# A graph network on one core: the lookup of 40 of 125 edge columns by TensorE taken out of the graph convolutions

## What is computed

```python
def gcn_conv(x, edge_index, W, b, num_nodes):
    ...
    norm = dinv[src_f] * dinv[dst_f]
    h = x @ W
    msg = h[src_f] * norm[:, None]
    out = jax.ops.segment_sum(msg, dst_f, num_segments=num_nodes)
    return out + b
```

## Time and profile before

| | |
|---|---|
| median of 3 runs | 33,800.93 us |
| range of the runs | 33,789.78 to 33,812.31 us |
| span of the profiled execution | 36,520.8 us |
| busy, share of the span: TensorE (PE) | 39% |
| VectorE (DVE) | 44% |
| ScalarE (ACT) | 7% |
| GpSimd (POOL) | 66% |
| mean granted TensorE clock | 0.635 |

### The profile page before, as it was taken

The page is one execution under the profiler, slowest core; times in us unless marked ns, Lnnn a source line. Parts: engine busy times, 40 slices in busy tenths (PEclk is TensorE's granted clock), DMA queues, the critical chain, the costliest instruction groups (busy, mean ns, idle before and its releaser), DMA issues. The chain is left out here.

```text
span 36520.8 us, 282841 instructions
## 1 busy us (share of the span) xinstructions
PE 14234.9 (39%) x71326; PEld 10717.5 (29%) x71326; DVE 16109.6 (44%) x34560; ACT 2593.5 (7%) x3901; POOL 24245.9 (66%) x29018
## 2 busy tenths in 40 slices
PE   1111100211110166664666524444444344266664
PEld 1111100111110155553555413222223222144443
DVE  3333337233333576663666513333334343344443
ACT  0000000000000000000000001001001000133230
POOL 6888841677774366664666566777687866477773
PEclk5555555555555577776778756666666666677775
DMA  2111112111112211110111110000000000100001
GB/s 49 15 15 15 15 37 106 19 23 21 23 23 52 89 29 29 28 29 14 29 29 30 24 11 10 13 10 10 12 11 13 11 12 8 60 14 15 14 14 51
DMA packets 1089471, 937.07 MB, mean 26 GB/s; under 512 B 580669, under 2 KB 1031893, under 8 KB 1063893
## 3 DMA queue, kind: packets, MB, share of 16 engines
q1 hardware_dynamic: 440100, 695.25, 6.4%
q0 software_dynamic: 646368, 201.76, 5.8%
q10 hardware_dynamic: 1872, 28.29, 0.2%
HBM read 497.08 MB, written 426.83 MB: 25 GB/s over the span
## 5 line engine op out<-in xcount | busy, mean ns | idle before, releaser
L1177 POOL DMA_INDIRECT messages<-se_M,se_rstage x2625 | 3029.5, 1154 | 1757.1 <-DVE se_M L1547 956.0
L1177 POOL DMA_INDIRECT messages<-pe_M,pe_rstage x2625 | 3132.7, 1193 | 1072.2 <-issue 791.8
L527 POOL DMA_INDIRECT se_G<-tab,se_stage x3125 | 3225.9, 1032 | 785.6 <-issue 783.3
L527 POOL DMA_INDIRECT g2g_G<-tab,g2g_stage x3125 | 3006.8, 962 | 1060.9 <-issue 779.0
L527 POOL DMA_INDIRECT g1g_G<-tab,g1g_stage x3125 | 3252.2, 1041 | 596.2 <-issue 582.3
L495 POOL DMA_INDIRECT c1c_G<-tab,c1c_stage x2125 | 2520.5, 1186 | 659.0 <-issue 640.0
L495 POOL DMA_INDIRECT c2c_G<-tab16b,c2c_stage x2125 | 2486.1, 1170 | 659.0 <-issue 640.8
L1076 DVE SCALAR_TENSOR_TENSOR g2gh_junk<-g2gh_pB,g2gh_src_f,earlier 128x128 f32<-128x128 f32 (+4 forms) x2625 | 1455.9, 614 | 2586.3 <-remote 1502.7
L1492 DVE TENSOR_TENSOR se_V<-se_pTV,s_b 128x160 f32 (+1 forms) x625 | 202.6, 324 | 4875.4 <-remote 3064.0
L767 PE MATMUL g1gh_acc<-g1gh_oh_hi,g1gh_oh_lo 128*128 128x100 bf16 x6250 | 546.5, 282 | 4133.4 <-DVE g1gh_oh_hi L747 3965.8
L1581 PE MATMUL se_pTV<-ident,se_pair 128*32 128x128 f32 x3125 | 598.3, 338 | 3904.0 <-DVE se_pair L1488 2600.5
(11 more groups left out here) (617 smaller groups left out, 36219.7 us busy)
## 6 DMA issues: line engine op xcount, KB each, us to landing
scans<-g1w_W SPq DMA_DIRECT2D x25, 3187.5 KB, 9.9
c1cm_row<-match SPq DMA_DIRECT2D x500, 128.0 KB
c2cm_row<-match SPq DMA_DIRECT2D x500, 128.0 KB
edges<-g2g_G SPq DMA_DIRECT2D x25, 2062.5 KB
g2w_G<-edges SPq DMA_DIRECT2D x25, 2062.5 KB, 11.6
scans<-g2w_W SPq DMA_DIRECT2D x25, 2062.5 KB, 7.3
g1g_G<-tab,g1g_stage POOLq DMA_INDIRECT x3125
g2g_G<-tab,g2g_stage POOLq DMA_INDIRECT x3125
```

Source lines behind the costliest of these rows:

```text
L527: g.indirect_dma_start(out=G[b][:, t, :], out_offset=None, in_=table, in_offset=bass.IndirectOffsetOnAxis(ap=stage[b][:, t:t + 1], axis=0) ...
L1177: g.indirect_dma_start(out=view, in_=M[b][:, DC + t, :], in_offset=None, out_offset=bass.IndirectOffsetOnAxis(ap=stage[b][:, t:t + 1], axis=0)
```

## The change

`gcn_gather` no longer makes a `Match`. All 125 columns are gathered by GpSimd through `stage_first` and `gather_and_stage`, as in `gat_gather`. VectorE and TensorE keep the side work alone, SP keeps the stores. Class `Match`, `match_rows`, the DRAM tensors `match` and the constants go.

```diff
-def gcn_gather(k, name, table, values, left, scans, carry, side):
+def gcn_gather(k, name, table, scans, carry, side):
...
-        stage = [c.sb(f"{name}_stage{b}", [P, PCH], I32) for b in range(2)]
+        stage = [c.sb(f"{name}_stage{b}", [P, CH], I32) for b in range(2)]
...
-        match = Match(k, c, name + "m", left)
         with k.nc.Block() as block:
             @block.gpsimd
             def _(g):
-                over_chunks(g, lambda i, b, j: gather_column_loop(
-                    g, k, i, j, b, table, G, stage, staged, stored, 16, got, k.src_i, PCH))
+                def chunk(i, b, j, first=False, last=False):
+                    gather_and_stage(g, i, j, b, table, G, stage, staged, stored, 16, got, k.src_i,
+                                     first=first, last=last)
+                stage_first(g, stage, staged, k.src_i)
+                chunk(0, 0, 0, first=True)
+                with g.Fori(0, PAIRS - 1) as j:
+                    chunk(2 * j + 1, 1, j)
+                    chunk(2 * j + 2, 0, j + 1)
+                chunk(NCH - 2, 1, PAIRS - 1)
+                chunk(NCH - 1, 0, PAIRS, last=True)
...
                 def chunk(i, b, j):
-                    match.heat(v, i, 0)
-                    v.wait_ge(stored[b], (j + 1) * 16)
-                    for m in range(max(NB + 1, side.groups)):
-                        if 1 <= m <= NB:
-                            match.mask(v, i, m - 1)
-                        if m + 1 < NB:
-                            match.heat(v, i, m + 1)
-                        if m < side.groups:
-                            side.vector(v, ch, i, side.ranges[0][0] + m)
-                        if 1 <= m <= NB:
-                            match.empty(v, G[b], i, m - 1)
-                    v.wait_ge(match.emptied, (i + 1) * NB + 2)
-                    v.wait_ge(got[b], (j + 1) * (16 * PCH))
+                    for m in range(side.groups):
+                        side.vector(v, ch, i, side.ranges[0][0] + m)
+                    v.wait_ge(got[b], (j + 1) * (16 * CH))
...
-            match_rows(k, "mr")
...
-            gcn_gather(k, name + "c", table, xs[:, :, :], agg, scan16, carry, side)
+            gcn_gather(k, name + "c", table, scan16, carry, side)
```

More of the change, by code:

```diff
@@ L45 @@
 D = 16
[L46 to L52, removed]
 H1, C1 = 3, 32
@@ L1012, in _ @@
             def _(pe):
-                match.tensor_first(pe)
                 side.tensor_first(pe)
                 def chunk(i, b, j):
[L1017 to L1025, removed]
+                    for m in range(side.groups):
+                        side.tensor_rows(pe, i, side.ranges[0][0] + m)
+                        side.tensor(pe, i, side.ranges[0][0] + m, False)
                 over_chunks(pe, chunk)
@@ L1035, in _, with chunk @@
                     s.sem_inc(stored[b], 16)
[L1037 to L1040, removed]
+                def chunk(i, b, j):
                     s.wait_ge(scanned, i + 1)
                     s.dma_start(rows(scans)[:, cols(i), :], G[b][:, :, :]).then_inc(stored[b], 16)
[L1043 to L1048, removed]
+                over_chunks(s, chunk)
                 s.wait_ge(stored[0], 16 * (PAIRS + 2))
@@ L1179, in scatter_column_loop @@
                              ).then_inc(sent[b], 16)
[L1182 to L1192, removed]
-            @block.tensor
-            def _(pe):
-                pe.wait_ge(staged, 1)
-                for i in range(NCH):
-                    mm = pe.transpose(turned[:, i * P:(i + 1) * P], src_f[:, i, :], k.ident[:, :])
-                mm.then_inc(transposed, 1)
-            @block.vector
-            def _(v):
-                ch = Chain(v, step)
-                v.tensor_copy(src_f[:, :, :], k.src_i[:, :].rearrange("p (i c) -> p i c", c=CH)[:, :, PCH:CH]
-                              ).then_inc(staged, 1)
-                v.wait_ge(transposed, 1)
-                ch(v.tensor_copy(node[:, :], turned[:, :]))
-                ch(v.tensor_scalar(part[:, :], node[:, :], 7, MR - 1, ALU.logical_shift_right, ALU.bitwise_and))
-                ch(v.tensor_copy(both[:, 1, :], part[:, :]))
-                ch(v.tensor_scalar(part[:, :], node[:, :], 10, 7, ALU.logical_shift_right, ALU.logical_shift_left))
-                ch(v.tensor_scalar(node[:, :], node[:, :], P - 1, None, ALU.bitwise_and))
-                ch(v.tensor_tensor(both[:, 0, :], node[:, :], part[:, :], ALU.add))
-            @block.sync
-            def _(s):
-                s.wait_ge(step, 6)
-                for h in range(2):
-                    s.dma_start(k.match[h].rearrange("i (c l) -> c i l", l=P),
-                                both[:, h, :].rearrange("c (i l) -> c i l", l=P)).then_inc(stored, 16)
-                s.wait_ge(stored, 32)
@@ L1905, in program @@
         scan16 = k.dram("scan16", [E + P, D])
-        k.match = [k.dram(f"match{h}", [NCH, PC * P], F16) for h in range(2)]
         k.carried = k.dram("carried", [P + 1, 51])
```

86 lines of the change are left out of this document (removed).

## The result

| | before | after | ratio |
|---|---|---|---|
| median (4 runs of each) | 33,806.27 us | 35,506.46 us | 1.0501 [1.0486, 1.0516] |
| range | 33,789.78 to 33,812.31 | 35,497.04 to 35,513.88 | |
| span of the profiled execution | 36,520.8 us | 35,512.1 us | |

The changed kernel is 5.0% slower, 1,700 us. The forecast was 35,420 us.

A forecast was written before the change was run, and what follows sets the result against it. VectorE and TensorE's matching loop was taken as the bound, GpSimd a chunk ahead. New blocks 8,570 less old 6,922 and 27 for `match_rows` give +1,621 on 33,801: 35,420 us, own range 34,950 to 35,850, 8 in 10 34,250 to 36,000.

The forecast's parts named there:

- column from start to start: GpSimd's gather loop after the change: one gather to the next, staging copy between, 1.32 us as in `g2g`.
- chunk without VectorE beside it: Convolution gather blocks after: 125 columns at 1.32 us give 165.0 us a chunk, before VectorE's stretch.
- stretch by VectorE: VectorE instructions reading two SBUF tiles lengthen GpSimd's work by 6.0 us a chunk, between 0 and 18.8.
- both blocks after: The two convolution gather blocks after the change: 4,285 us each, 8,570 us together, at 171.5 us a chunk.
- both blocks before, timed: The two old gather blocks in the timed run: 6,922 us, the profile's 7,983 less 1,061 of remote waits.
- difference: Timed run, after minus before: new blocks 8,570, less old blocks 6,922 and 27 for `match_rows`, +1,621 us.
- artefact of recording: Claim that long remote waits in the gather blocks come from recording slowing TensorE to a beat, absent from timed runs.
- remote waits: VectorE's idle time behind TensorE in the old gather blocks: 595 and 633 us, 76 waits, 2.2 us of each true.
- rival 1: TensorE really needs the remote waits' time; old blocks stay 7,983 us, difference +560, time 34,360 us; chance 0.17.
- the beat: TensorE's slow fixed pace for small matmuls after dense bursts, for example one every 1.38 us, blamed on recording.
- Rival 2: Recording makes GpSimd's instructions dear: timed column 1.13 us, chunk 148, blocks 7,400 against 7,983; 33,190 us; chance 0.06.
- Rival 3: VectorE stretches GpSimd in the new blocks as in `g1g`: 186.5 us a chunk, +2,341, 36,140 us; chance 0.11.

The follow-up runs named there:

- e1: The kernel before, unedited, recorded once more: 33,672.48 us, span 33,670.7 us.
- e4: The changed kernel with place counting of both convolutions run in a block of its own ahead of the gathers: 38,853.36 us.
- e2: The changed kernel with each chunk's 125 staged indices copied in one go instead of column by column: 35,064.98 us, ratio 1.0416 to before.
- e3: The kernel before with 20 of 125 columns looked up by TensorE instead of 40: 34,183.93 us, ratio 1.0154 to before.
- e12: The changed kernel, unedited, run again in the third series: 38,953.50 us, ratio 1.0167 to before in that series.
- e5: The changed kernel, unedited, run again in the second series: 37,806.04 us, ratio 1.033 to before in that series.

## Why the prediction was right, and where its reasons were not

**The bound and the terms.** Each line is a step of the prediction; measured values come from the profile of after and from `e1` and `e4`.

| step | predicted | measured |
|---|---|---|
| column from start to start | 1.32 us | 1.318 (median) |
| chunk without VectorE beside it | 165.0 us, and 0.5 for the loop | 168.1 (with the scans beside it) |
| stretch by VectorE | 6.0 with the scans (0 to 18.8) | 6.8 and 5.9, by place counting alone |
| chunk | 171.5 us | 174.9 and 174.0 |
| both blocks after | 8,570 us | 8,725 |
| both blocks before, timed | 6,922 (6,525 to 7,300) | 6,778 in `e1` |
| `match_rows` | -27 us | -27 |
| difference | +1,621 us | +1,841 by profiles, +1,700 by medians |

GpSimd is the bound after and VectorE waits for landings; removing the match frees nothing that was late; both as forecast. The time came out 86 us above the forecast.

The range of 34,950 to 35,850 is narrower than its own bounds make it: 168 us a chunk with 7,300 for the old blocks gives 34,876 us, 178 with 6,525 gives 36,131.

**What was mis-sized.** Two terms, both to the same side. First the chunk of 165.0 us. 125 x 1.32 multiplies the usual distance and misses what happens once a chunk. After, ahead of the 114th gather of each of the 25 chunks, there is this, GpSimd:

```profile
13571.48 0.96 POOL L520 DMA_INDIRECT c1c_G<-tab,c1c_stage  x1 [0.15 <-issue]
13572.44 0.20 POOL L516 COPY c1c_stage<-src_i 128x1 int32 x1
13575.59 0.96 POOL L520 DMA_INDIRECT c1c_G<-tab,c1c_stage  x1 [2.94 <-issue]
```

2.94 us in which GpSimd waits for nothing that is shown. It stands at the same gather in `g1g`, `g2g` and `se`, in the profile of before too, where it lay open to be read. It makes 2.94 - 0.15 = 2.8 of the 3.1 us between 165.0 and 168.1. It goes with the number of gathers: `e2`, with no copies between them, has it at the 114th of each chunk as well,

```profile
12839.57 0.95 POOL L488 DMA_INDIRECT c1c_G<-tab,c1c_stage  x1 [3.21 <-issue]
```

and the chunks of 81, 85 and 105 gathers never have it. Second the old blocks, 6,922 against 6,778: I left 2.2 us for each of the 76 disturbed waits, but waits under other names were longer too. TensorE's waits for the folded match (`c1cm_out` on `c1cm_kept`) are 265.0 us in the first recording of `c1c` and 55.4 in `e1`. Together (155 + 144) less the 80 us of the sheaf are +219 on +1,621, the 1,841 of the two profiles. The medians differ by 141 us less, because before has 33,806 us in the first comparison and 33,672 in `e1`. In which stages these 134 us lie no kept trace shows; if in the old blocks, then 6,922 was nearly right for the timed runs. That the forecast missed by 86 us and not by some 220 is luck: both mis-sized terms made the loss too small, and a kernel before that was slower there than in `e1` took most of it back.

**The step that failed.** "I read them as an artefact of recording." The half that fed the sum held: the remote waits are not in the 33,800 us, the difference of the medians isn't that of the spans, and rival 1, by which they were TensorE's true work, fell with `e1`. The other half doesn't hold. `e1` is a full recording of the same kernel at 33,672 us, and after, `e2`, `e3` and `e4` are full recordings without the beat as well. The 7 runs of before in series 1 are as short as `e1`; all 13 of series 2 and all 13 of series 3 are longer, by 3,000 and 4,600 us in the median. From this half came a forecast that failed: after's span should have been 37,000 to 37,500 us, since its recording would have the beat too. It was 35,512.1.

The Trainium skill (NOTIFIC — the notification-queue block, section 7.1) says that the block's inner pipeline holds back its producers rather than lose a record inside it. No run here shows the block. The disturbed traces do show VectorE released late behind TensorE's bursts of small matmuls (`e12`). But a recording of the same kernel with as many instructions (`e1`) passed without it, so that rule alone doesn't tell when it occurs.

**Rivals.** Rival 2 (faster) needed a column under 1.277 us; after it is 174.9 / 125 = 1.40 with all that a chunk holds, and even the loop of `e2` has 166.3 / 125 = 1.33. Rival 3 (the pace of `g1g`, 186.5 us) asked for 18.8 us of stretch; it is 6.8. Chunks above 186.5 us did occur, in `e5` and `e12`, by another mechanism than the one named: TensorE's late releases.

**What stays open.** What puts TensorE on its slow beat in two of three series, on the same chip in one case. Every kernel has it there, so it belongs to no change. It costs the kernel before more than the changed one: between the two recordings of before the blocks `c1c` and `c2c` account for 1,205 us, between after and `e5` the same stages account for some 300. The old blocks have more than twice as many matmuls; that this is the reason isn't shown. Whether the beat would be there without a recording can't be told, since no unrecorded run is on hand. What the stop at the 114th gather is stays open as well; nothing tried splits a chunk to avoid it. No version tried beats the kernel before; the best form of the change, `e2`, is still 4.2% slower.

## What to carry to other kernels

Before a profile's waits are costed, hold its span against the timed runs. Where they differ by several per cent, take a second profile of the same kernel first: a cause argued from one disturbed recording can carry a right sum for a wrong reason. Look at the single times behind a mean or a median: here a mean of 29.8 us was made of 0.3 and 62, and medians of disturbed chunks of the convolutions lay up to 20 us from their means. A loop's price is its whole period divided by its turns, not the usual distance of two instructions times their number: here that was 3 us of 168. When work is moved from a busy pair of engines to a third that is itself within 6% of setting the pace (129 of 137 us), little of it is hidden; but it can be cheaper than its price, where the work that goes had held that third engine. Here 40 columns at 1.25 us are 50 us, and the chunk grew by 28.9 us (`e2`), because 8 us were to spare, each of the 85 gathers became 0.2 us shorter, and 3 us came in with the stop: 50 - 8 - 17 + 3 = 28.

## What the hardware showed that I had not expected

- The same program took 33,666, 36,699 and 38,316 us in three series, steady within each, and in the changed kernel with busy times of TensorE and VectorE in block `c1c` equal to a tenth of a per cent, only the waits behind TensorE longer.
- A comparison of two SBUF tiles on VectorE holds an indirect DMA's issue on GpSimd by about 0.6 us once (0.96 to 1.59). When such comparisons follow one another without idle time, a 128x125 index copy waits for the end of all 93: 61.7 us instead of 0.29, in 24 of 24 such cases.
- GpSimd stops for about 2.9 us before the 114th gather of every chunk of 125, with copies between the gathers or without, and with nothing named as the releaser; chunks of 105 gathers and fewer don't have it.
- A one-column copy between two gathers costs 0.067 us of pace, though it takes 0.20 us by itself.
